# Other slots for the steps of a four-part model kernel, with the table functions of ScalarE grouped, slots of their own for the first and the last row, and the first norm ahead of the weight work

## The reference

```python
x = x + mamba(layernorm(x))      # inner norm with gamma, beta; returns its input + y @ W_out
x = x + ffn(layernorm(x))        # ternary weights
x = x + mingru(layernorm(x))
x = x + ffn(layernorm(x))        # the same ternary weights

# mamba: xi, z = split(h @ W_in)                              256 inner features each
#        u = silu(causal conv of 4 taps over xi + b_conv)
#        dt_r, B, C = split(u @ W_x); dt = softplus(dt_r @ W_dt + b_dt)
#        for each of 16 states n: s_t = exp(dt_t * A_n) * s_{t-1} + dt_t * u_t * B_t,n ; y_t += s_t * C_t,n
#        return input + ((y + u * Dskip) * silu(z)) @ W_out
# ffn:   t(w) = sign(w) where |w| > half the mean of |w|, else 0
#        r(x) = x / rms(x); h = gelu(r(x) @ t(w_up).T); return r(h) @ t(w_down).T
# mingru: i = silu(x @ W1 + b1); skip = silu(x @ W2 + b2)     512 features
#        z = sigmoid(i @ Wz + bz); c = i @ Wh + bh; h_t = (1 - z_t) * h_{t-1} + z_t * c_t
#        return (skip + h) @ Wo + bo
```

## Time and profile before

| | us |
|---|---|
| median of 3 runs | 964.21 (962.77 to 964.9) |
| the profiled execution | 965.4, its span 963.3 |
| busy in the span: PE | 743.3 (77%) |
| DVE | 686.2 (71%) |
| ACT | 677.6 (70%) |
| POOL | 596.0 (62%) |
| first scan of row 0 starts at | 51.16 |
| last scan of row 7 starts at | 838.89 |

### The profile page before, as it was taken

One profiled execution on the slowest core, in us unless ns is written; L12 is line 12 of the kernel. 1 busy time (PEld: TensorE's weight loads), 2 busy tenths in 40 slices (PEclk: granted clock), 3 DMA queues, 4 the chain that ended last, 5 costly groups with the idle time before them and its releaser, 6 DMA issues.

```text
span 963.3 us, 12301 instructions
## 1 busy us (share of the span) xinstructions
PE 743.3 (77%) x4058; PEld 616.7 (64%) x4058; DVE 686.2 (71%) x961; ACT 677.6 (70%) x980; POOL 596.0 (62%) x378
## 2 busy tenths in 40 slices
PE   2354647678978798789887897879778988896885
PEld 1144445557866587667766786668656777686674
DVE  1179978687968697769867896869786998743231
ACT  3665566778697968888798779796888486634413
POOL 2488756765678568666778577756875667513412
PEclk9985667879978997989978997899989988998895
DMA  1341211111111011111211111111111111000000
GB/s 43 89 160 51 67 44 55 44 46 43 47 44 57 32 46 55 46 44 44 56 46 33 56 56 42 48 34 47 42 46 45 49 51 33 12 1 1 12 0 12
DMA packets 35184, 42.78 MB, mean 44 GB/s; under 512 B 7457, under 2 KB 17074, under 8 KB 35122
## 3 DMA queue, kind: packets, MB, share of 16 engines
q1 hardware_dynamic: 35122, 42.00, 14.4%
HBM read 39.63 MB, written 2.36 MB: 44 GB/s over the span
## 4 chain that ended last, share of the span: by engine, by line
PE 37%; ACT 27%; DVE 17%; issue 12%; POOL 5%; SPq 1%; ACTq 0%; DMA 0%; POOLq 0%; DVEq 0%
DVE state L853 8%; PE work L1034 6%; PE work L1036 5%; PE work L1035 5%; PE y_ps L1121 5%; ACT L629 5%; DVE state L860 3%; PE work L1212 3%; PE work L1204 3%; ACT dA L630 3%; ACT dA L629 3%; POOL wide L458 3%; PE c_ps L1112 2%; ACT n_tok L645 1%; ACT wide L669 1%
## 5 line engine op out<-in xcount | busy, mean ns | idle before, releaser
L439 POOL TENSOR_TENSOR inflow<-dtu,b_all 128x1024 f32<-128x1024 f32 x128 | 313.3, 2448 | 123.2 <-DVE state L853 90.3
L853 DVE TENSOR_TENSOR_SCAN state<-dA,inflow 128x1024 f32<-128x1024 f32 x128 | 292.7, 2286 | 78.7 <-ACT dA L630 69.3
L860 DVE TENSOR_TENSOR state<-state,c_ps 128x1024 f32<-128x1024 f32 x128 | 155.4, 1214 | 3.8 <-PE c_ps L1112 1.7
L1121 PE MATMUL y_ps<-ident,state 128*128 128x128 f32 x1024 | 155.7, 303 | 0.0
L629 ACT ACTIVATE dA<-dt,decay_c 128x512 f32<-128x512 f32 x128 | 88.6, 692 | 88.9 <-DVE state L853 85.3
L1121 PEld LDWEIGHTS y_ps<-ident,state 128*128 128x128 f32 x1024 | 139.8, 158 | 16.3 <-issue 6.5
L1112 PE MATMUL c_ps<-xd,pick 128*128 128x512 f32 x128 | 68.9, 538 | 87.8 <-DVE state L860 87.4
L1034 PE MATMUL work<-in_hi,wzh_hi 128*128 128x512 f32 x256 | 108.2, 423 | 26.4 <-ACT skip_f L682 17.5
L1035 PE MATMUL work<-in_hi,wzh_lo 128*128 128x512 f32 x256 | 104.5, 408 | 0.0
L1036 PE MATMUL work<-in_lo,wzh_hi 128*128 128x512 f32 x256 | 104.3, 408 | 0.0
L1112 PEld LDWEIGHTS c_ps<-xd,pick 128*128 128x128 f32 x128 | 27.2, 212 | 111.6 <-DVE state L860 93.4
(11 more groups left out here) (161 smaller groups left out, 1600.7 us busy)
## 6 DMA issues: line engine op xcount, KB each, us to landing
b_all<-b_scratch SPq DMA_DIRECT2D x128, 256.0 KB, 3.1
x_tok<-in_x SPq DMA_DIRECT2D x8, 256.0 KB, 3.7
out_x<-x_tok SPq DMA_DIRECT2D x8, 256.0 KB, 3.6
wide<-in_Wz SPq DMA_DIRECT2D x1, 1024.0 KB, 6.7
wide<-in_Wh SPq DMA_DIRECT2D x1, 1024.0 KB, 9.0
...
```

The costliest lines, as they stand in the source:

```text
L439: pool.tensor_tensor(inflow[:, n % 2, :, :], dtu[:, :, :], b_all[:, n % RING, :].unsqueeze(1).broadcast_to([P, HALVES, SEQ]), ALU.mult).th ...
L853: dve.tensor_tensor_scan(flat(state[:, g % 3, :, :]), flat(dA[:, :, :]), flat(inflow[:, n % 2, :, :]), 0.0, ALU.mult, ALU.add).then_inc(s_ ...
L860: dve.tensor_tensor(state[:, g % 3, :, :], state[:, g % 3, :, :], c_ps[:, :].unsqueeze(1).broadcast_to([P, HALVES, SEQ]), ALU.mult).then_i ...
L1121: last = pe.matmul(y_region(j, h), state[:, g % 3, h, cols(j)], ident[:, :], is_transpose=True, start=False, stop=(n == STATE - 1), skip_g ...
```

## The change

1. All four slot tables and `BANK` have other numbers, most of them by a quarter to three quarters of a slot. `silu_u` and the gelus of ffn "a" now stand close together (slots 4 to 5.75 of a period), `in0` to `in7` and `ln_set` come in slots 11 to 11.5, all ahead of decay 13 and of the softplus (12.5), `silu_z` goes to slot 13.75. The squares of "d" all stand ahead of decay 11, and its three sums in one quarter. `read` goes from 0.25 to 0.75, `c` from -0.25 to 0, `acc` from 0.75 to 1.25.
2. A table `MOVED` gives 78 steps of row 0 and 111 steps of row 7 slots of their own; `due` and `latest` now look in lists of absolute slots.
3. The explicit load ahead of `silu_u` is gone; a load is placed in front of it where needed.
4. `prepare_mix` and `decay_rates` no longer stand at slot 14 of row -2: the one follows `apply`(0), the other `mix_h`(0). gamma and beta have a semaphore of their own. TensorE's waits for weights stand at each use.
5. Row 0's three convs and its first inflow are done by VectorE instead of GpSimd.

```diff
 ACT_AT = {
-    "decay": -1, "h_tok": -17.75, "h": -16.75, "taps0": -15, "taps1": -15, "z_copy0": -9.75, "z_copy1": -11,
-    "silu_u": -9, "silu_z": -9.25, "ln_set": -2, "xd": -7, "softplus": -3.75, "gated0": 16, "gated1": 16.5,
-    "apply1": 18, "apply2": 25.25, "apply3": 38, "hi1": 18.25, "hi2": 26.25, "hi3": 38.75, "a.gelu0": 20,
-    "d.gelu0": 40, "a.square0": 21, "d.square0": 41, "in0": 27, "in4": 27.5, "a.gelu1": 21.75, "d.gelu1": 40,
-    "a.square1": 21.75, "d.square1": 41, "in1": 27, "in5": 27.5, "a.gelu2": 21.75, "d.gelu2": 40.5,
-    "a.square2": 22, "d.square2": 42, "in2": 27, "in6": 27.5, "a.gelu3": 21.75, "d.gelu3": 40.5,
-    "a.square3": 22.25, "d.square3": 42, "in3": 27, "in7": 28, "gate0": 29.5, "gate1": 30, "gate2": 31,
-    "gate3": 34,
+    "decay": -1, "h_tok": -17.75, "h": -16.5, "taps0": -13.75, "taps1": -14.75, "z_copy0": -6.5,
+    "z_copy1": -9.25, "silu_u": -10.75, "silu_z": -2.25, "ln_set": -4.5, "xd": -6.25, "softplus": -3.5,
+    "gated0": 16.75, "gated1": 16, "apply1": 18.75, "apply2": 26, "apply3": 38.25, "hi1": 19.25, "hi2": 26.25,
+    "hi3": 38.75, "a.gelu0": 20, "d.gelu0": 39.25, "a.square0": 20, "d.square0": 40, "in0": 27, "in4": 27.25,
+    "a.gelu1": 20, "d.gelu1": 39.75, "a.square1": 20, "d.square1": 41, "in1": 27.25, "in5": 27.25,
+    "a.gelu2": 21.5, "d.gelu2": 40.25, "a.square2": 21.75, "d.square2": 41, "in2": 27.25, "in6": 27.25,
+    "a.gelu3": 21.75, "d.gelu3": 40.25, "a.square3": 22.25, "d.square3": 41, "in3": 27.25, "in7": 27.5,
+    "gate0": 30, "gate1": 31.25, "gate2": 31.25, "gate3": 33.25,
 }
...
+MOVED = {
+    ("ACT", "a.gelu2", 0): 20, ("ACT", "a.gelu3", 0): 20.25, ("ACT", "a.square3", 0): 22.75,
...
+def times(eng, at):
+    return {op: [STATE * b + MOVED.get((eng, op, b), at[op]) for b in range(ROWS)] for op in at}
...
-            for dst, src in ((gamma_c[:, :], gamma.rearrange("(p a) -> p a", a=1)),
-                             (beta_c[:, :], beta.rearrange("(p a) -> p a", a=1)),
-                             (win_f, W_in),
+                             (beta_c[:, :], beta.rearrange("(p a) -> p a", a=1))):
+                sp.dma_start(dst, src, allow_slow_non_contiguous=True).then_inc(s_affine, 16)
+            for dst, src in ((win_f, W_in),
...
-                for b in due(r, s, ACT_AT["silu_u"]):
-                    act.preload_act_table(ACT.Silu)
+                for b in due(r, s, ACT_ON["silu_u"]):
                     mix_silu_u(b)
...
             for r, s in slots():
-                if (r, s) == (-2, 14):
-                    prepare_mix()
...
+                for b in due(r, s, DVE_ON["apply"]):
                     mix_apply(b)
+                    if b == 0:
+                        prepare_mix()
+                for k in (1, 2, 3):
+                    for b in due(r, s, POOL_ON["conv%d" % k]):
+                        if b == 0:
+                            mix_conv(dve, b, k)
...
+                for b in due(r, s, DVE_ON["dtu"]):
                     mix_dtu(b)
+                    if b == 0:
+                        mix_inflow(dve, 0, 0)
```

More of the change, by code:

```diff
@@ L60 @@
+    "z_copy1": -9.25, "silu_u": -10.75, "silu_z": -2.25, "ln_set": -4.5, "xd": -6.25, "softplus": -3.5,
[6 rows of a table added]
 }
 DVE_AT = {
-    "scan": 0, "read": 0.25, "norm": -19.75, "apply": -17.5, "xd_lo": -5.75, "dt": -2.25, "dtu": -1.5,
[4 rows of a table removed]
+    "scan": 0, "read": 0.75, "norm": -25.75, "apply": -18, "xd_lo": -5.25, "dt": -2.25, "dtu": -1.75,
+    "gate": 16.25, "x1": 17.75, "x2": 25, "x3": 37.25, "a.ms": 24.25, "d.ms": 43.75, "d.out": 44.25,
[4 rows of a table added]
 }
 PE_AT = {
-    "c": -0.25, "acc": 0.75, "skip": 0.5, "abs": 2.5, "up_t": 10.25, "down_t": 11, "ht": -16.25, "xi0": -14.75,
[6 rows of a table removed]
+    "c": 0, "acc": 1.25, "skip": 0.75, "abs": 2.25, "up_t": 10.75, "down_t": 9, "ht": -15.75, "xi0": -13.5,
[6 rows of a table added]
@@ L76 @@
 }
 BANK = {
[5 rows of a table removed]
[5 rows of a table added]
 }
 ONCE = ("abs", "up_t", "down_t")
+MOVED = {
[3 rows of a table added]
+    ("ACT", "h_tok", 0): -19.25, ("ACT", "h", 0): -17.5, ("ACT", "in1", 0): 27, ("ACT", "in2", 0): 27,
+    ("ACT", "in3", 0): 27, ("ACT", "in4", 0): 27, ("ACT", "in5", 0): 27, ("ACT", "in7", 0): 29,
+    ("ACT", "ln_set", 0): -4.75, ("ACT", "silu_u", 0): -10, ("ACT", "silu_z", 0): -7.75,
+    ("ACT", "softplus", 0): -5, ("ACT", "taps0", 0): -15.5, ("ACT", "taps1", 0): -15.5, ("ACT", "xd", 0): -6.5,
+    ("ACT", "z_copy0", 0): -10, ("ACT", "z_copy1", 0): -10, ("DVE", "a.ms", 0): 24.5, ("DVE", "apply", 0): -15,
+    ("DVE", "dtu", 0): -2, ("DVE", "dt", 0): -2.5, ("DVE", "factors1", 0): 18.75, ("DVE", "factors3", 0): 38.25,
+    ("DVE", "gate", 0): 16.5, ("DVE", "hid0", 0): 33.5, ("DVE", "hid2", 0): 36, ("DVE", "in_hi0", 0): 27.75,
+    ("DVE", "in_hi1", 0): 28, ("DVE", "in_hi2", 0): 28.5, ("DVE", "in_hi3", 0): 28.5, ("DVE", "lo1", 0): 20,
+    ("DVE", "new0", 0): 31.75, ("DVE", "new2", 0): 35.25, ("DVE", "norm", 0): -18.25, ("DVE", "read", 0): 0.25,
+    ("DVE", "stats1", 0): 18.75, ("DVE", "x1", 0): 18.5, ("DVE", "xd_lo", 0): -4.5, ("PE", "a.down", 0): 23.5,
[4 rows of a table added]
+    ("POOL", "a.rms", 0): 24, ("POOL", "a.sum1", 0): 21.25, ("POOL", "base", 0): -11,
+    ("POOL", "conv1", 0): -10.5, ("POOL", "conv2", 0): -10.25, ("POOL", "conv3", 0): -10,
+    ("POOL", "d.rms", 0): 43.75, ("POOL", "h_lo", 0): -8, ("POOL", "in_lo0", 0): 27.25,
+    ("POOL", "inflow", 0): -2, ("POOL", "keep1", 0): 33, ("POOL", "keep2", 0): 33.5, ("POOL", "root1", 0): 18.5,
+    ("POOL", "root", 0): -15.25, ("ACT", "a.gelu0", 7): 19.25, ("ACT", "a.gelu1", 7): 19.5,
[6 rows of a table added]
+    ("ACT", "gated1", 7): 15.75, ("ACT", "h_tok", 7): -17.25, ("ACT", "hi2", 7): 25.75, ("ACT", "in0", 7): 27.5,
+    ("ACT", "in1", 7): 27.5, ("ACT", "in2", 7): 27.5, ("ACT", "in3", 7): 27.75, ("ACT", "in4", 7): 28.75,
+    ("ACT", "in5", 7): 28.75, ("ACT", "in6", 7): 33.5, ("ACT", "in7", 7): 34.5, ("ACT", "silu_u", 7): -10.5,
+    ("DVE", "a.ms", 7): 22.75, ("DVE", "d.ms", 7): 45.25, ("DVE", "d.out", 7): 47, ("DVE", "dtu", 7): -2,
+    ("DVE", "factors1", 7): 18.75, ("DVE", "factors3", 7): 38, ("DVE", "gate", 7): 16.5,
[3 rows of a table added]
+    ("DVE", "new2", 7): 33, ("DVE", "new3", 7): 34.25, ("DVE", "norm", 7): -25.5, ("DVE", "stats3", 7): 35,
[10 rows of a table added]
+    ("POOL", "a.sum3", 7): 22, ("POOL", "base", 7): -10, ("POOL", "conv1", 7): -12.25,
+    ("POOL", "d.rms", 7): 44.75, ("POOL", "d.sum1", 7): 44.5, ("POOL", "d.sum2", 7): 44.5,
+    ("POOL", "d.sum3", 7): 44.75, ("POOL", "in_lo0", 7): 27.75, ("POOL", "in_lo3", 7): 30,
+    ("POOL", "inflow", 7): -1.5, ("POOL", "keep0", 7): 33.25, ("POOL", "keep1", 7): 34,
+    ("POOL", "keep3", 7): 35, ("POOL", "root3", 7): 43.5, ("POOL", "root", 7): -21.75,
+    ("POOL", "x2b", 7): 30.75,
+}
@@ L90, in slots, with due, latest @@
             yield r, q / PHASES
-def due(r, s, at):
-    b = r - (at - s) / STATE
-    return [int(b)] if b == int(b) and 0 <= b < ROWS else []
-def latest(r, s, at):
-    return min(int((STATE * r + s - at - 1 / (2 * PHASES)) // STATE), ROWS - 1)
+def due(r, s, on, n=0):
+    return [b for b in range(ROWS) if on[b] + n == STATE * r + s]
+def latest(r, s, on):
+    return sum(at < STATE * r + s for at in on) - 1
 def sequence():
@@ L296, in cols, with mix_conv, mix_inflow @@
             return slice(j * P, (j + 1) * P)
+        def mix_conv(eng, b, s):
+            if s == 1:
+                evacuated(eng, b, "xi0")
+                evacuated(eng, b, "xi1")
+            else:
+                eng.wait_ge(s_conv, (TAPS - 1) * b + s - 1)
+            eng.tensor_tensor(u[:, :, s:SEQ], u[:, :, s:SEQ], tapped[s - 1][:, :, 0:SEQ - s], ALU.add
+                              ).then_inc(s_conv, 1)
+        def mix_inflow(eng, b, n):
+            g = STATE * b + n
+            eng.wait_ge(s_bring[n % RING], 16 * (STATE // RING * b + n // RING + 1))
+            eng.wait_ge(s_dtu, b + 1)
+            if g == 1:
+                eng.wait_ge(s_inflow, 1)
+            wait(eng, s_scan, g - 1)
+            eng.tensor_tensor(inflow[:, n % 2, :, :], dtu[:, :, :],
+                              b_all[:, n % RING, :].unsqueeze(1).broadcast_to([P, HALVES, SEQ]), ALU.mult
+                              ).then_inc(s_inflow, 1)
         block = ctx.enter_context(nc.Block())
-        W_MIX, W_TAIL = 16 * (8 + 5 + 3), 16 * 10
+        W_MIX, W_TAIL = 16 * (6 + 5 + 3), 16 * 10
         @block.sync
@@ L1070, in mix_zin @@
                 p = "zin%d" % i
+                evacuated(pe, b, "ht")
+                pe.wait_ge(s_hlo, b + 1)
+                pe.wait_ge(s_win, 1)
                 bank_free(b, p)
```

200 lines of the change are left out of this document (92 added, 108 removed), and 62 rows, old and new, of tables (BANK, DVE_AT, MOVED, PE_AT).

## The result

The changed kernel takes 894.36 us (median of 4 runs, 889.54 to 895.51) against 964.34 (962.77 to 964.9): ratio 0.927, 95% interval 0.9235 to 0.9309. So 70 us went; 908 was predicted, within its range. The profiled execution took 889.54, the fastest of the four and 4.8 under their median: its own difference to the profiled execution of before is 75.9.

What follows compares the result with a forecast made beforehand. No engine is full over a row; the bound moves inside it, with ScalarE and its table loads filling the long slots. 32.5 + 7 + 1.5 + 6.7 + 0 + 8 = 55.7 us off 965.4 gave 909.7, predicted as 908; range 895 to 925.

Steps and rivals of the forecast that it cites:

- the rival in which the row closes fully: Steady rows: loads, `in0`'s earlier start and recovered TensorE clock all count, 9.5 us a row, 889 us in all; chance 0.18.
- Prologue: Before the first scan: earlier first norm, row 0's convolutions and first inflow on VectorE; 6.7 us less.
- Row 0: First row of scans: two table loads fewer, 1.5 us less.
- Steady row: Rows 2 to 6: parts sum to 8.0 us, TensorE takes over some; 6.5 us less a row, 32.5 in all.
- Loads in the long slots: Slots of decays 13 and 14: seven ScalarE table loads become three, silu added; 4.1 us less a row.
- 2.3* of slots 4 to 10: Middle of a steady row: one table load and `silu_z` leave ScalarE, 2.3 us less a row.
- Wait in front of `in0`: TensorE's wait for GpSimd's sums of squares ahead of `in0` goes; 1.6 us less a row.
- Row 1: Second row of scans: eight table loads fewer, same share from the long slots; 7 us less.
- Row 7: Last row of scans: keeps its table loads; 0 gained, 2 us either way.
- The end: After the last scan: earlier a.down, squares, `norm2` and gates, d.sumsq between d.down's halves; 8 us less.
- The slower rival: Every scan: later reads stall TensorE's queue; at 0.55 us a slot the kernel takes 978 us; chance 0.09.
- The table does not carry over: ScalarE, long slots: case against `ln_set`'s table serving softplus and decays 13, 14 without loads; chance 0.03, no size given.

Runs made afterwards that it cites:

- a_pool0: Changed kernel with row 0's three convolution steps and first inflow back on GpSimd; 900.17 us, ratio 0.9334.
- a_ln_back: Changed kernel with `ln_set` back at -2, behind the softplus (row 0 as in the change); 924.21 us, ratio 0.9589.
- a_none: Changed kernel with `MOVED` empty, so rows 0 and 7 have the slots of all others; 905.64 us, ratio 0.9389.
- a_hid: Changed kernel with the GRU scans of blocks 2 and 3 moved to 36.75, behind the read of scan 4; 907.19 us, ratio 0.9412.
- b_group: Kernel before with two slots changed: `in7` to 27.5 and `ln_set` to -4.5, ahead of decay 13 and the softplus; 936.93 us, ratio 0.9713.
- b_gsums: b_group plus the down projection's squares 2 and 3 at 41 and its sums on GpSimd at 41.5; 930.08 us, ratio 0.9649.
- b_cread: b_gsums plus the changed kernel's later `c`, `acc` and `read`, with gates and what follows up to 0.75 slot later; 970.35 us, ratio 1.006.
- a_read: Changed kernel with each scan's read at 0.5 instead of 0.75 in all rows but row 0; 917.26 us, ratio 0.952.

## Why the prediction came out as it did

By the profiled executions 55.7 us were forecast and 75.9 went; by the medians 56 and 70. The measured 894.36 lies in the range, but nearer to the rival in which the row closes fully (889) than to 908. The direction and the places of the gain were forecast; the steady row and row 0 were sized too small. Step by step:

- *Prologue*: 6.7 forecast, 7.2 measured (51.16 to 43.94), by the forecast's own means. n_tok runs at 7.38, the three convolutions on VectorE from 21.16 to 24.90, silu_u at 24.93. a_pool0 puts 3.5 us of it on VectorE's convolution and inflow (2.8 and 0.9 predicted).
- *Row 0*: 1.5 forecast, 6.5 measured. The step "Row 0 loses two: 1.5" counted loads over the row and did not ask where they stand: `ln_set` and the softplus of row 1 stand in row 0's last slots. By the starts of the scans 6.0 of the 6.5 us lie between scan 12 and scan 14: 14.29 before, 8.32 after. With only that `ln_set` put back (a_ln_back) these two intervals take 10.73 and the row 80.85, so two loads make some 2.4 to 3.2 of it. Row 0's own slots are not the cause: a_none has 8.32 there too. Which of the general slots gives the rest stays open. The row's total is loose by itself: a_hid, whose order up to the end of row 0 is that of the kernel after, has 80.59.
- *Steady row*: 6.5 forecast, 9.0 measured on average (10.0, 9.0, 7.9, 8.7, 9.3), 8.3 against a_pool0 and a_none. The term was mis-sized, in three places. *Loads in the long slots*, 4.1: b_group gives 4.2 in row 3, a_ln_back 5.4; about right, though b_group takes out five loads, 6.4 us by the same price, and does not move the silu. The *2.3* of slots 4 to 10 came as 4.5 in one interval (7 to 8) and went again in two others: from scan 4 to 5 VectorE is busy throughout, and from scan 8 to 9 it has 3.58 us of work in 7.58 and waits 2.61 for TensorE's sums and 1.40 for c_ps. The stretch is 1.0 longer. *Wait in front of `in0`*, 1.6: real as a wait, worth 0.3 a row as time (b_gsums). Missing from the working is what b_group leaves in the last six intervals, 5.1 us (37.01 to 31.93). The two profiles shown above point to TensorE's order: no hole ahead of c_ps, so matmuls of 0.39 us and not 0.63, so gates in time; no experiment isolates it, and this is not shown. I had this in favour of a rival ("closed holes also shorten its own matmuls") and priced it only there. That rival, 9.5 us a row, was nearer for the steady row than the forecast.
- *Row 1*: 7 forecast, 9.0 measured, the same error.
- *Row 7*: 0 forecast, 0.4 measured.
- *The end*: 8 forecast, 7.4 measured (122.10 to 114.72). The size is right as a sum of two things that I did not separate: the general slots cost 3.1 there (125.20 in a_none), the own slots gain 10.5. It is also partly luck: with the same order there, other executions had up to 118.47, a gain of 3.6. The bare stretch at the very end did go: the 1.97 us from ms_d to the output now lie beside matmuls of the down projection (PE L1252, 2.03 us from 881.75). VectorE in the kernel after, against the last two of the earlier trace rows:

```profile
881.93 0.16 DVE L988 TENSOR_SCALAR ms_d<-work 128x4 f32<-128x4 f32 x1 [11.78 <-PE work L1262]
...
883.90 1.13 DVE L999 SCALAR_TENSOR_TENSOR x_tok<-work,rscale_d,x_tok 128x128 f32<-128x128 f32 x4 [0.29 <-PE work L1252]
```

- *The slower rival* did not happen. In the old order of the other steps a later read with its c does cost 40 us (b_cread), over half of the 70 that I gave it, but the rival's mechanism, TensorE waiting for reads, grew by 12 us only; VectorE waiting between scan and read grew by more. In the new order an earlier read costs 23 us (a_read). My 0.09 rested on "the scan after the read waits mostly for dA" and on the DVE work being the same in another order; b_cread shows that neither makes a late read free.
- *The table does not carry over*: refuted, by the timeline at 387.44.
